# A convolution with sampled sign weights: the last two units of weights in two parts, M added by VectorE, and a first triple of six half-image tiles

## What is computed

```python
A = m * m + jnp.sum(z * z, axis=0) / SCALE            # z: 8 draws, SCALE = 100
inv = lax.rsqrt(A)
w = (rv @ (z * inv))[0] + m * inv                      # rv: 8 random factors
bw = jnp.sign(w)
ba = jnp.sign(_gn(x))
out = x + conv(ba, bw, padding=1) * alpha
```

## Time and profile before

| | us |
|---|---|
| median of 3 runs (lowest, highest) | 502.14 (501.99, 502.36) |
| the profiled execution | 501.43 |
| its span, first to last instruction | 499.70 |
| TensorE busy | 468.5 (94%) |
| VectorE busy | 408.0 (82%) |
| ScalarE busy | 321.4 (64%) |
| mean granted TensorE clock | 0.991 of full speed |

### The profile page before, as it was taken

The page is one execution under the profiler, slowest core; times in us unless marked ns, Lnnn a source line. Parts: engine busy times, 40 slices in busy tenths (PEclk is TensorE's granted clock), DMA queues, the critical chain, the costliest instruction groups (busy, mean ns, idle before and its releaser), DMA issues.

```text
span 499.7 us, 8225 instructions
## 1 busy us (share of the span) xinstructions
PE 468.5 (94%) x2638; PEld 388.9 (78%) x2638; DVE 408.0 (82%) x849; ACT 321.4 (64%) x547; POOL 24.3 (5%) x70
## 2 busy tenths in 40 slices
PE   0887989999999999999999999999999999999994
PEld 0433557888888888888888888888888888888993
DVE  1544879998898988988888988889889889888695
ACT  1665788677767667676677667676666775673330
POOL 8200000000000000000000000000000000000100
PEclk9988999999999999999999999999999999999999
DMA  7999999065956856857659568568577596653264
GB/s 234 399 399 395 336 347 372 0 246 205 308 216 242 271 208 239 293 205 275 249 202 321 203 247 285 194 238 300 194 267 258 199 317 225 226 194 133 108 237 167
DMA packets 47213, 124.37 MB, mean 249 GB/s; under 512 B 3792, under 2 KB 6608, under 8 KB 47184
## 3 DMA queue, kind: packets, MB, share of 16 engines
q1 hardware_dynamic: 47184, 124.01, 68.9%
HBM read 72.62 MB, written 51.38 MB: 248 GB/s over the span
## 4 chain that ended last, share of the span: by engine, by line
PE 82%; SPq 6%; DVE 5%; DMA 4%; issue 1%; ACT 1%; DVEq 0%; ACTq 0%
PE conv_ps L380 80%; SPq L270 5%; DMA m_sb<-in_L_conv_M_dram 4%; DVE bn L667 2%; PE conv_ps L332 1%; ACT whole L445 1%; PE conv_ps L346 1%; DVE low L759 1%; DVE whole L751 0%; PE conv_ps L335 0%; DVE bn L691 0%; ACT low L450 0%; DVE chan L680 0%; SPq L271 0%; DVE chan L676 0%
## 5 line engine op out<-in xcount | busy, mean ns | idle before, releaser
L380 PE MATMUL conv_ps<-signs,wts 128*128 128x492 f32 (+5 forms) x1944 | 419.0, 377 | 2.0 <-ACT signs L488 1.4
L380 PEld LDWEIGHTS conv_ps<-signs,wts 128*128 128x128 f32 x1944 | 363.7, 188 | 57.2 <-issue 1.4
L501 ACT ACTIVATE part<-conv_ps 128x492 int32<-128x492 f32 (+3 forms) x108 | 61.6, 570 | 133.2 <-PE conv_ps L380 130.5
L488 ACT ACTIVATE signs<-x_sb,shift,rstd 128x784 fp32r<-128x784 f32 x128 | 126.0, 1035 | 5.0 <-DVE shift L738 5.0
L751 DVE SCALAR_TENSOR_TENSOR whole<-conv_ps,part 128x492 int32<-128x492 f32 (+3 forms) x108 | 71.0, 657 | 42.8 <-PE conv_ps L380 34.7
L759 DVE SCALAR_TENSOR_TENSOR low<-whole,conv_ps 128x492 f32<-128x492 int16 (+3 forms) x108 | 70.7, 655 | 3.7
L775 DVE SCALAR_TENSOR_TENSOR x_sb<-whole,alpha_sb,x_sb 128x784 f32<-128x784 int16 (+1 forms) x68 | 66.8, 983 | 0.9
L775 DVE SCALAR_TENSOR_TENSOR x_sb<-low,alpha_sb,x_sb 128x784 f32<-128x784 f32 (+1 forms) x68 | 66.7, 981 | 0.0
L691 DVE BATCH_NORM_STATS2 bn<-x_sb 128x6 f32<-128x392 f32 x116 | 59.3, 553 | 0.3 <-issue 0.3
L472 ACT ACTIVATE unread<-x_sb 128x784 bf16<-128x784 f32 x58 | 49.1, 846 | 0.5 <-DMA x_sb<-in_x_dram 0.5
L474 ACT ACTIVATE unread<-x_sb 128x784 bf16<-128x784 f32 x58 | 49.0, 845 | 0.0
(11 more groups left out here) (52 smaller groups left out, 156.1 us busy)
## 6 DMA issues: line engine op xcount, KB each, us to landing
x_sb<-in_x_dram SPq DMA_DIRECT2D x64, 784.0 KB, 5.7
out_dram<-x_sb SPq DMA_DIRECT2D x63, 784.0 KB, 3.8
x_sb<-in_L_conv_Z_dram SPq DMA_DIRECT2D x56, 288.0 KB, 7.4
x_sb<-in_L_conv_Z_dram SPq DMA_DIRECT2D x16, 144.0 KB, 4.1
m_sb<-in_L_conv_M_dram SPq DMA_DIRECT2D x7, 288.0 KB, 8.3
out_dram<-x_sb SPq DMA_DIRECT2D x2, 392.0 KB, 2.5
m_sb<-in_L_conv_M_dram SPq DMA_DIRECT2D x2, 144.0 KB, 4.0
alpha_sb<-in_L_conv_alpha_dram SPq DMA_DIRECT2D x2, 0.5 KB, 2.4
```

Source lines behind the costliest of these rows:

```text
L380: mm = pe.matmul(sums_of_tile(b, at, skip, drop), wts[:, ch, kh * KW + kw], e, start=n == 0, stop=n == PRODUCTS - 1, skip_group_check=True)
L488: nc.scalar.activation(o, x_sb[:, slot_of(t, j), h].rearrange("p (a b) -> p a b", b=W), ACT.Sign, bias=shift[:, t % BODY, j, h:h + 1], sca ...
L501: nc.scalar.activation(part[:, at, 0:columns(b)], conv_ps[at][:, 0:columns(b)], ACT.Copy, scale=-FRACTION / PACK, bias=FRACTION / 2).then_ ...
```

## The change

- The three small loads (rv, alpha) are issued from ScalarE's queue instead of SyncE's. Image 0 is loaded one load of weights earlier.
- M is no longer added through TensorE: VectorE adds it to the sum in PSUM (`unit_qm`), writes the result to `w`, and multiplies there later. `one` and its making go away. A buffer of weights is free for SyncE only after this addition (`qm_done`), which for unit c stands behind the squares of unit c + 1.
- The last load is split by draws: four draws of both units and M first, then the other four. Units 14 and 15 (TWIN and TWIN + 1) go side by side in two parts (`first_q`, `second_q`, `first_a`, `second_a`, `part_squares`).
- The three early packings share one PSUM bank; the late ones pack the first half of the output channels before the last signs (`pack(n, 0)`).
- The first triple is done image by image, in six half-image tiles (FIRST) instead of five tiles: nine products of the first ahead of the last packing and nine of the second right behind it. All tile numbers behind it are one higher, and banks rotate by one (`bank`).
- EARLY is 3: the statistics of images 3 to 5 are shared by ScalarE and VectorE too.

The core of the diff:

```diff
+    TWIN = UNITS - 2
...
-    EARLY = TRI * STAT_LEAD
+    EARLY = TRI
...
-        wt_ps = [psum(f"wt_ps{i}", [P, 512], F32) for i in range(2)]
-        a_ps = conv_ps[0:2]
-        q_ps = conv_ps[2:5]
-        taps_ps = [wt_ps[0], wt_ps[1], wt_ps[0], wt_ps[1], wt_ps[0], a_ps[1]]
+        wt_ps = [psum(f"wt_ps{i}", [P, 512], F32) for i in range(3)]
+        a_ps = conv_ps[3:5]
+        q_ps = [conv_ps[2], wt_ps[0], wt_ps[1]]
+        taps_ps = [wt_ps[2], wt_ps[2], wt_ps[2], wt_ps[2], wt_ps[0], wt_ps[1]]
...
+        FIRST = tuple(TILES + i for i in range(2 * TRI))
...
+            return (b + 1) % TILES
...
-            sp.dma_start(rv_sb[:], rv.to_broadcast([P, K])).then_inc(consts_loaded, 16)
-            for h in range(HALVES):
-                sp.dma_start(alpha_sb[:, h:h + 1], alpha_v[h]).then_inc(consts_loaded, 16)
...
-                need(sp, q_done, 2 * (c - ZR + 1))
+                need(sp, qm_done, 2 * (c - ZR + 1))
...
-                parts = 1 if c < LOADS - 1 else 2
-                for u in range(parts):
-                    to = slice(u * CW, (u + 1) * CW) if parts == 2 else slice(0, 2 * CW)
-                    cols = slice(b * 2 * CW + to.start, b * 2 * CW + to.stop)
-                    loaded = z_loaded[c % ZR] if u == 0 else last_loaded
-                    for kq in range(K // KQ):
-                        for j in range(KQ):
-                            sp.dma_start(z_sb[:, c % ZR, kq, j, to], z_v[kq, h, :, :, j, cols]).then_inc(loaded, 16)
-                    sp.dma_start(m_sb[:, c % ZR, to], m_v[h * P:(h + 1) * P, cols]).then_inc(loaded, 16)
+                cols = slice(b * 2 * CW, (b + 1) * 2 * CW)
+                for kq in range(K // KQ):
+                    loaded = last_loaded if c == LOADS - 1 and kq == 1 else z_loaded[c % ZR]
+                    for j in range(KQ):
+                        sp.dma_start(z_sb[:, c % ZR, kq, j], z_v[kq, h, :, :, j, cols]).then_inc(loaded, 16)
+                    if kq == 0:
+                        sp.dma_start(m_sb[:, c % ZR], m_v[h * P:(h + 1) * P, cols]).then_inc(loaded, 16)
...
-                if c == LOADS - 5:
+                if c == LOADS - 6:
...
-                need(pe, w_done, c - 2)
+                need(pe, qm_done, c - 2)
...
-                    mm = pe.matmul(q_ps[c % 3][j * QUAD:(j + 1) * QUAD, 0:CW], one[:, j * QUAD:(j + 1) * QUAD],
-                                   m_sb[:, c // 2 % ZR, cols], start=False, stop=True)
...
+            first_q(TWIN)
+            unit_a(TWIN - 1)
+            first_q(TWIN + 1)
+            first_a(TWIN)
+            first_a(TWIN + 1)
+            second_q(TWIN)
+            second_q(TWIN + 1)
+            second_a(TWIN)
+            second_a(TWIN + 1)
+            pe.wait_ge(dve_wts_done, 2)
+            pe.wait_ge(w_sign_done, TWIN)
+            pack(TAP_ROUNDS, 0)
+            pe.wait_ge(qm_done, TWIN)
+            pack(TAP_ROUNDS + 1, 0)
+            pe.wait_ge(qm_done, TWIN + 1)
+            pack(TAP_ROUNDS + 2, 0)
+            pe.wait_ge(act_wts_done, 1)
             pe.wait_ge(signs_done, 1)
-            pe.wait_ge(act_wts_done, 2)
-            pe.wait_ge(dve_wts_done, 1)
-            pe.wait_ge(a_full, UNITS - 1)
-            products(0, 0, 0, 0, TAPS)
-            pe.wait_ge(a_full, UNITS)
+            products(0, FIRST[0], 0, 0, TAPS)
+            pe.wait_ge(w_sign_done, UNITS)
             for n in range(TAP_ROUNDS, HALVES * TAP_ROUNDS):
-                pack_taps(n)
-            pe.wait_ge(act_wts_done, HALVES * TAP_ROUNDS - 1)
+                pack(n, 1)
+            products(0, FIRST[1], 1, 0, TAPS)
+            def first_triple():
+                pe.wait_ge(act_wts_done, 3)
+                first_products(0, FIRST[0], 0, 1, 0, TAPS)
+                first_products(0, FIRST[1], 1, 1, 1, TAPS)
+                pe.wait_ge(act_wts_done, 4)
+                rest_products(0, FIRST[0], 0, 0)
+                rest_products(0, FIRST[1], 1, 1)
+                for i in range(2, 2 * TRI):
+                    first_products(0, FIRST[i], i % TILES, i // 2 + 1, i)
+                    if i > 2:
+                        rest_products(0, FIRST[i - 1], (i - 1) % TILES, i - 1)
...
+            act.dma_start(rv_sb[:], rv.to_broadcast([P, K])).then_inc(consts_loaded, 16)
+            for h in range(HALVES):
+                act.dma_start(alpha_sb[:, h:h + 1], alpha_v[h]).then_inc(consts_loaded, 16)
...
+            unit_inv(TWIN - 2)
+            unit_sign(TWIN - 3)
+            part_squares(TWIN, 0)
+            unit_sign(TWIN - 2)
+            part_squares(TWIN + 1, 0)
+            unit_inv(TWIN - 1)
+            part_squares(TWIN, 1)
+            unit_sign(TWIN - 1)
+            part_squares(TWIN + 1, 1)
+            unit_inv(TWIN)
+            unit_inv(TWIN + 1)
+            unit_sign(TWIN)
+            unit_sign(TWIN + 1)
             for n in range(TAP_ROUNDS, HALVES * TAP_ROUNDS):
                 copy_taps(n)
-            deviation(1, 0, 1, 2)
-            image_signs(0, 1, 0, 1)
+            def first_triple():
+                fraction(FIRST[0], 0, 0)
+                deviation(1, 0, 1, 2)
+                fraction(FIRST[1], 1, 1)
+                image_signs(0, 1, 0, 1)
+                sums(0, 1, 0)
+                fraction(FIRST[2], 2, 2)
+                deviation(2, 0, 2, TRI)
+                image_signs(0, 2, 0, 2)
+                sums(0, 1, 1)
+                fraction(FIRST[3], 3, 3)
+                sums(0, 1, 2)
+                fraction(FIRST[4], 4, 4)
+                deviation(TRI, 1, 0, TRI)
+                image_signs(1, TRI, 1, 0)
+                fraction(FIRST[5], 0, 5)
+                image_signs(1, TRI, 1, 1)
+                sums(0, 2, 0)
+                sums(0, 2, 1)
+                image_signs(1, TRI, 1, 2)
+                sums(0, 2, 2)
...
+            def unit_qm(c):
+                dve.wait_ge(q_done, c + 1)
+                need(dve, w_sign_done, c - QR + 1)
+                m = m_sb[:, c // 2 % ZR, c % 2 * CW:(c % 2 + 1) * CW]
+                nc.vector.tensor_tensor(w[:, c % QR], q_ps[c % 3][:, 0:CW], m, ALU.add).then_inc(qm_done, 1)
...
-                dve.wait_ge(q_done, c + 1)
-                need(dve, w_sign_done, c - QR + 1)
-                nc.vector.tensor_tensor(w[:, c % QR], q_ps[c % 3][:, 0:CW], inv[:, c % QR],
-                                        ALU.mult).then_inc(w_done, 1)
+                dve.wait_ge(qm_done, c + 1)
+                nc.vector.tensor_tensor(w[:, c % QR], w[:, c % QR], inv[:, c % QR], ALU.mult).then_inc(w_done, 1)
...
+            unit_w(TWIN - 2)
+            part_squares(TWIN, 0)
+            unit_m_squares(TWIN)
+            unit_qm(TWIN - 1)
+            unit_a_sum(TWIN - 1)
+            copy_taps(2)
+            part_squares(TWIN + 1, 0)
+            unit_m_squares(TWIN + 1)
+            unit_w(TWIN - 1)
+            part_squares(TWIN, 1)
+            part_squares(TWIN + 1, 1)
+            unit_qm(TWIN)
+            unit_qm(TWIN + 1)
+            unit_a_sum(TWIN)
+            unit_a_sum(TWIN + 1)
+            unit_w(TWIN)
+            unit_w(TWIN + 1)
+            stats_of_both(1, 0, 4)
+            group_steps(1, 0, 2, BODY + 1)
+            stats_of_both(2, 0, 1)
+            stats_of_both(2, 1, 4)
+            group_steps(2, 0, TRI, BODY + 2)
+            def first_triple():
+                high_sum(0, 0, FIRST[0], 0, 0)
+                bounded(2, 0, 2, TRI)
+                low_sum(0, 0, FIRST[0], 0, 0)
+                negative_mean(2, 0, 2, TRI, BODY + 2)
+                sums(0, 1, 0, lambda: tile_sums(0, 0, FIRST[1], 1, 1))
+                sums(0, 1, 1, lambda: None)
+                sums(0, 1, 2, lambda: tile_sums(0, 0, FIRST[2], 2, 2))
+                group_steps(TRI, 1, 2 * TRI, 1)
+                high_sum(0, 0, FIRST[3], 3, 3)
+                bounded(TRI, 1, 0, TRI)
+                low_sum(0, 0, FIRST[3], 3, 3)
+                negative_mean(TRI, 1, 0, TRI)
+                for j in range(TRI):
+                    sums(0, 2, j, lambda: None)
...
```

293 lines of the change are left out of this document (155 added, 138 removed).

## The result

The changed kernel takes **509.82 us** (median of 4 runs, 507.30 to 510.83); the kernel before, measured beside it, takes 502.19 (501.99 to 502.36). The ratio is 1.0145, 95% interval 1.0104 to 1.0185. It is slower, as forecast, but by 7.6 us and not by 3.0. The profiled execution took 510.68 us (span 509.0), 9.25 more than the 501.43 of before. Traces are compared by these own times.

The account below looks back on a forecast made before the run. TensorE bounds the kernel, with ScalarE's fraction equally critical at the second triple's first tile. Profiled 501.43 + 1.3 (later landmark) + 1.7 (clock) = 504.4, other terms 0; as median 505.1 us, range 500.0 to 507.5.

Parts of the forecast that it names:

- the mechanism in the second triple: Second triple's first tile: TensorE waits 5.6 us for ScalarE's fraction, half clock follows; +1.3 and +1.7 us.
- ScalarE between the first fraction and the landmark: ScalarE's queue up to the second triple's first fraction: 24.4 us of work plus 3.9 of waits, ending at 101.65.
- the landmark: Moment TensorE starts the last four products of the second triple's first tile: forecast 101.7 against 100.42, +1.3 us.
- The clock: TensorE's granted clock falls to half in the 5.6 us idle gap: +1.7 us, bounds 0.8 and 2.5.
- Rival (c): Second triple: the clock stays up over TensorE's gap, leaving +1.3 alone, 503.4 us; chance 0.10.
- Behind the last sign: From the last sign's end at 69.25, packing and 14 more products, to tile 0's first fraction at 73.35.
- Everything starts 1.39 us earlier: Weights' loads: with small loads off SyncE, the stream moves 1.39 us earlier, units 12 and 13 there at 54.49.
- TensorE waited for data at each landing: Weights' stage, kernel before: the reason given for earlier loads moving the seventh load's arrival from 55.88 to 54.49.
- M is added by VectorE. Term: 0: Weights' stage: reload gate keeps about 3 us of slack, so 0; if lost, 1 to 3 us.
- The tail from the landing to the last sign: From units 12 and 13 landing to the last sign's end: 14.8 us against 16.1 before, ending at 69.25.
- rival (d): Weights' tail not shortened: stream unmoved, reload waiting for M, or half rate; 1.4 to 3 us later, 506.5 to 508; chance 0.10.
- the page that I cited on loads from a second engine: Small loads on ScalarE's queue: saves only sequencer time; were the stream not moved, the sum would be 1.4 us higher.

Follow-up runs that it names:

- Experiment 3: Changed kernel with sums of images 7 and 8 on VectorE alone, fractions ahead of sums, third triple's group step one tile earlier: 502.53 us, ratio 1.0004.
- experiment 5: Changed kernel with only the fraction of the second triple's first tile moved ahead of image 7's sums, no work removed: 507.50 us, ratio 1.0100.
- experiment 1: Changed kernel with GpSimd's memset of the signs buffer waiting until VectorE has made `mix`: 507.83 us, ratio 1.0127.
- experiment 9: Kernel of 4 with M added by TensorE again and VectorE's additions gone: 500.74 us, ratio 0.9973.
- experiment 11: Kernel of 6 with ten spare TensorE products, results unread, before the waits at five landings: 498.02 us, ratio 0.9918.
- experiment 10: Kernel of Experiment 3, memset not moved, with VectorE's addition of M for each load's second unit ahead of the next squares: 501.44 us, ratio 0.9986.
- 2: Changed kernel with the three small loads issued by SyncE ahead of the weights again: 509.80 us, ratio 1.0152.
- 4: Changed kernel with both repairs, the edits of Experiment 3 and experiment 1 together: 499.88 us, ratio 0.9958.
- 6: Kernel of 4 with VectorE's addition of M for each load's second unit ahead of the next unit's squares: 498.63 us, ratio 0.9943.
- experiment 8: Kernel of 4 with the last load's split by draws undone, so engines wait for all draws of the last two units: 500.64 us, ratio 0.9974.
- experiment 7: Kernel before with one part of the change alone, its three small loads issued by ScalarE: 501.24 us, ratio 0.9995.
- 12: Kernel of 6 with 20 spare TensorE products before the waits at five landings: 500.38 us, ratio 0.9963.

## Why the prediction was wrong

The direction was right, and so was the mechanism in the second triple. The time was 4.7 us off in the median and 6.3 in the profiled run (510.68 against 504.4), and these are the steps:

- **ScalarE between the first fraction and the landmark: right.** 28.6 us against 28.3, and the wait of 5.45 us against 5.6, named `part`. Experiment 3 removes it, experiment 5 moves it.
- **The clock: right, the size within its bounds.** It fell in the wait and cost 2.45 us against 1.7 (0.8 to 2.5). Rival (c) falls, and experiment 3 shows the full clock where the wait is gone.
- **Behind the last sign: right.** First fraction 4.17 us after the end of the last sign, 4.1 forecast.
- **"Everything starts 1.39 us earlier": the step that failed.** Units 12 and 13 landed at 58.05, not at 54.49. I moved the issues on SyncE's queue but not the small loads' own readers: I did not ask what VectorE makes from them, nor what GpSimd does meanwhile. The data of the first load did come 1.1 us earlier (11.76 against 12.82), but `mix` was done only at 15.66. The term was too large besides. With `mix` in time TensorE begins on them at 55.57 (experiment 1), at 55.43 without VectorE's addition in the gate (9), and at 55.19 at the earliest (11), against 55.88 before: of the 1.39 us 0.3 to 0.7 arrive. "TensorE waited for data at each landing" was a wrong reading: before, its rows name a DMA at five of the seven loads.
- **"M is added by VectorE. Term: 0": the second half of the same failure.** I gave the reload gate 3 us of slack. SyncE waited for the addition 8.5 us in two pieces, and 6.8 us in experiment 1, where VectorE starts in time: the slack was not there. What the gate costs by itself is not shown. In experiment 1 the landing is only 0.14 us behind that of experiment 9, which has no such gate. Where TensorE starts late, the landing is at 57.38 to 58.80 (the changed kernel, 3, 5, 10); where `mix` is in time and the gate is there, at 55.57 to 57.28 (1, 2, 4, 6, 8). So much of the 3.6 us goes with the late start, and how much differs from trace to trace. In the kernel before the late start cost nothing (experiment 7), but its stream began earlier there too; that the gate is what makes it cost here is possible, and experiment 10 did not show it. Whether the addition itself is worth its place is open at 0.86 us (experiment 9); with spare products it is, at 2.7 us (experiment 11).
- **The tail from the landing to the last sign: right at full clock only.** I had 14.8 us; experiment 1 has 14.65 (55.57 to 70.22); the trace of the changed kernel has 16.3, with PEclk at 0.81 and 0.85 from 55 to 65. All traces with VectorE's addition fall in two groups by TensorE's row at this landing: 14.6 us where its 16 products take 1.18 us (experiments 1, 2, 5, 6, 8, 11, 12), 16.1 to 16.3 where they take 1.73 to 2.15 (the changed kernel, 3, 4, 10). I had named half rate among the last units in rival (d) and did not carry it in the sum.

The errors of the last three steps add up: 3.6 + 1.6 = 5.2 us on the first fraction, which is 78.55 − 73.35; with 0.3 on ScalarE's stretch this is the landmark's 107.2 against 101.7. **Rival (d) is what happened**, and it had a chance of 0.10 and a price of 1.4 to 3 us; the price should have been that of the stage's whole fall-back, and the range should have reached past 508. I had the words "a reload waits for the added M" and took it for unlikely because of slack that I had worked out with every engine in time. The landmark's 5.5 us and 0.75 us more for the clock are the profiled run's 6.3; that the median is only 4.7 off is the draw of the runs.

As to the page that I cited on loads from a second engine (the Trainium skill, DMA: Bandwidth & Descriptors, section "Issuing engines are not separate DMA queues"): the saving of SyncE's time did show, 1.1 us on the first data, but what ScalarE issued was there 2.4 us later than the same loads from SyncE (6.50 against 4.14). Before, these loads went ahead of the first weights; now both are issued at 0.8 us. Whether the issuing engine makes them late, or the weights' loads that start with them, no run tells.

What stays open: the price of the late start and of the gate in the changed kernel itself, and how the two share it. Between experiments 3 and 4 it is 2.65 us, between 10 and 6 2.8; in the changed kernel four to five runs with some 3 to 4 us of spread don't tell.

## What to carry to other kernels

Moving a small load moves whoever reads it: follow the value to its first reader and look at what GpSimd is doing there, and put a long memset behind the short passes of VectorE that everything waits for. Slack of a gate is to be worked out over the whole queue of the engine that opens it, and with that engine late too. And where a change takes work from TensorE in a stage that waits for data, expect the time to spread: look at every run, not at one trace, and a few spare products in the waits may give back more than they take.

## What was new about the hardware

- A GpSimd memset of 8.82 us held two VectorE tensor_scalar passes of together 0.39 us for 8.08 us (8.80 in experiment 7), while a tensor_tensor pass that takes 0.75 us elsewhere took 0.76 beside such a memset.
- The same three small loads were there 2.4 us later when ScalarE issued them beside SyncE's first weights than when SyncE issued them ahead of these (6.50 and 6.47 against 4.14 and 4.16 us).
- The run-to-run spread goes with TensorE's idle time at the landings. Ten spare products of together 1.8 us at five landings brought it from 3.8 to 0.2 us (experiments 6 and 11). With M's 64 products on TensorE it was 0.55 us, without them 4.2 (9 and 4), but there the gate changed too, and the kernel before, which has these products, spread 2.2 us over 20 runs. The mean granted clock goes the same way without fixing the time: in experiment 8 it is 0.991 in the fastest run (498.16) and 0.984 in all six from 500.56 to 502.68.
